# Gated cross-attention and top-2 expert layer on one core: tile phases from five, six and eight groups, tiles of 256 and 128 rows, and an earlier opening

## What is computed

```
x = x + tanh(g_xattn) * attention(layernorm(x), ctx, ctx, Wq..bo, mask)     # 16 heads of 8
x = x + tanh(g_ffn)   * experts(layernorm(x))

experts(x):                                   # 4096 rows
    scores    = x @ gate_w + gate_b           # 8 experts
    p, e      = softmax of the top 2 scores
    h[e]      = relu(x @ w1[e] + b1[e])       # 128 -> 512
    y[e]      = h[e] @ w2[e] + b2[e]          # 512 -> 128
    out       = p[0] * y[e[0]] + p[1] * y[e[1]]
```

## Time and profile before

| | |
|---|---|
| runs shown | 463.8, 464.79, 465.64 us (median 464.79) |
| the profiled execution | 462.04 us, its span 460.2 us |
| mean granted TensorE clock | 0.951 |
| busy: PE, PE weight load, DVE, ACT, POOL | 403.7, 327.5, 284.3, 271.4, 273.6 us |
| DMA | 72.55 MB, mean 158 GB/s |

### The profile page before, as it was taken

How to read it: one execution, slowest core, us unless ns; L and a number is a source line. 1 busy time by engine, 2 the same in 40 slices (tenths; PEclk the granted TensorE clock), 3 DMA queues, 4 the chain that set the end, 5 groups by cost and what they waited for, 6 DMA issues and landing times.

```text
span 460.2 us, 12345 instructions
## 1 busy us (share of the span) xinstructions
PE 403.7 (88%) x4299; PEld 327.5 (71%) x4299; DVE 284.3 (62%) x1034; ACT 271.4 (59%) x824; POOL 273.6 (59%) x297
## 2 busy tenths in 40 slices
PE   1799999999999999999998759999959999999700
PEld 1466677778777777777775639998848999999700
DVE  2678796788887878888889533446403333333257
ACT  1388777878787878877785413444313444444244
POOL 8743365277797887987746603777774445555500
PEclk9999999999999999999999768999979999999955
DMA  3999999830000000000000183677385777776188
GB/s 79 232 317 412 413 411 335 157 64 22 25 13 28 19 13 27 14 25 26 15 25 20 43 257 114 214 230 236 116 245 177 226 229 226 228 234 206 78 261 292
DMA packets 48154, 72.55 MB, mean 158 GB/s; under 512 B 8053, under 2 KB 32637, under 8 KB 48093
## 3 DMA queue, kind: packets, MB, share of 16 engines
q1 hardware_dynamic: 43549, 62.32, 44.3%
q0 software_dynamic: 4544, 9.45, 5.7%
HBM read 41.83 MB, written 34.66 MB: 166 GB/s over the span
## 4 chain that ended last, share of the span: by engine, by line
PE 74%; DVE 6%; POOL 6%; DMA 5%; issue 3%; ACT 2%; SPq 2%; POOLq 0%; ACTq 0%; DVEq 0%
PE U L747 8%; PE S L769 7%; PE S L635 7%; PE T L747 7%; PE O L769 7%; PE S L645 6%; PE O L675 6%; PE T L653 5%; PE O L685 5%; PE U L653 5%; POOL zs L996 3%; PE E L627 2%; DMA yg<-res 2%; ACT P L841 2%; PE E L616 2%
## 5 line engine op out<-in xcount | busy, mean ns | idle before, releaser
L841 ACT ACTIVATE P<-S,nmax 128x120 f32<-128x120 f32 x512 | 137.1, 413 | 41.0 <-DVE nmax L1137 41.0
L1007 POOL DMA_INDIRECT res<-yo,dpos x78 | 74.7, 957 | 75.8 <-DVE yo L1307 67.3
L1137 DVE TENSOR_REDUCE nmax<-S 128x4 f32<-128x480 f32 x128 | 75.2, 650 | 20.1 <-PE S L645 15.0
L996 POOL DMA_INDIRECT zs<-z,posu x64 | 64.6, 1009 | 36.4 <-PE O L685 15.5
L884 ACT ACTIVATE H<-U,wbuf 128x256 f32<-128x256 f32 x82 | 34.4, 470 | 53.9 <-PE U L747 53.8
L635 PE MATMUL S<-mb_r,I_r 128*128 128x480 f32 x128 | 61.7, 486 | 4.4 <-ACT P L841 3.9
L884 ACT ACTIVATE H<-T,wbuf 128x256 f32<-128x256 f32 x74 | 31.0, 470 | 51.5 <-PE T L747 51.5
L969 POOL TENSOR_SCALAR Kb<-Kt,hm 128x480 f32<-128x480 f32 x32 | 47.3, 1486 | 19.8 <-ACT Kt L868 6.9
L957 POOL TENSOR_SCALAR z<-X,mv,rstd 128x128 f32<-128x128 f32 x64 | 50.4, 793 | 10.9 <-PE O L685 7.1
L747 PE MATMUL U<-zT,wbuf 128*128 128x256 f32 x164 | 45.4, 402 | 1.6 <-ACT H L884 1.6
L747 PE MATMUL T<-zT,wbuf 128*128 128x256 f32 x148 | 39.6, 391 | 7.3 <-DMA wbuf<-wpk 5.2
(11 more groups left out here) (166 smaller groups left out, 693.5 us busy)
## 6 DMA issues: line engine op xcount, KB each, us to landing
wbuf<-wpk SPq DMA_DIRECT2D x39, 578.0 KB
zs<-zero SPq DMA_DIRECT2D x1, 17952.0 KB, 60.4
zin<-zs SPq DMA_DIRECT2D x39, 132.0 KB, 3.4
yg<-res SPq DMA_DIRECT2D x16, 256.0 KB, 3.7
wpk<-in_w SPq DMA_DIRECT2D x1, 2048.0 KB, 56.4
wpk<-in_w SPq DMA_DIRECT2D x8, 256.0 KB, 8.8
out<-X SPq DMA_DIRECT2D x16, 128.0 KB, 3.4
ctx_sb<-in_ctx SPq DMA_DIRECT2D x1, 1440.0 KB, 17.0
```

Source lines behind the costliest of these rows:

```text
L841: ins = nc.scalar.activation(P[:, n % 4, j, :], a[:, j * LK:(j + 1) * LK], ACT.Exp, bias=nmax[:, n % 4, j:j + 1])
L996: nc.gpsimd.indirect_dma_start(out=zs, out_offset=bass.IndirectOffsetOnAxis(ap=posu[:, F, k, i:i + 1], axis=0), in_=z2[:, F % 2, i, :], in ...
L1007: nc.gpsimd.indirect_dma_start(out=res, out_offset=bass.IndirectOffsetOnAxis(ap=dpos[:, n % NDP, h:h + 1], axis=0), in_=yo[:, n % NYO, h, ...
L1137: v.tensor_reduce(nmax[:, n % 4, :], Sb[n % NHG][:, 0:HG * LK].rearrange("p (j k) -> p j k", j=HG), AX_X, ALU.max, negate=True).then_inc(m ...
```

## The change

- `SB` becomes (5, 1, 2): tables are made after five, six and eight groups. The first phase has 12 tiles, the second 4, the third 15, and a fourth has `SINGLES` = 9 tiles of 128 rows. That is 31 tiles of 256 rows and 9 of 128, 71 halves. Rows that an expert has over its full tiles of 256 go to a tile of 256 or of 128.
- `tile_order` puts two tiles of 128 rows behind every three of the third phase. For a tile of 128 rows `first_product` computes all four chunks for its 128 rows.
- The stage is one sequence without an opening per phase. It opens in round 31 (`OPEN`), before the values of that round; the steps use banks S0 and S1 in turn, the first products T and U in turn.
- `DRAIN_PAIRS`: rounds 32 to 37 hold 4, 3, 3, 2, 2, 2 halves; 16 halves are placed.
- POOL scatters groups 5, 6 and 7 in rounds 31/32, 34 and 37, and results one round later.
- Six weight buffers. Rows and weights of the first 16 tiles are loaded without waiting for the last group.
- The start: loads are split over more semaphores, the first context is loaded earlier, z1 of group 0 and three of four masked keys move from POOL to DVE, V, tanh, b2 and bo move behind the first scores, into round 0.

```diff
-SB = (6, 2)
+SB = (5, 1, 2)
...
-NTB = [FULL, max((2 * NG * TOK + NE * (TS - 1)) // TS - FULL, (2 * SB[1] * TOK + 2 * NE * (TS - 1)) // TS)]
+FULL = [(2 * n * TOK - NE * (TS - 1)) // TS for n in LAST[:-1]]
+HS = 128
+SINGLES = NE + 1
+PAIRED = ((2 * NG * TOK + NE * (HS - 1)) // HS - SINGLES + 1) // 2
+NTB = [n - b for n, b in zip(FULL + [PAIRED], [0] + FULL)] + [SINGLES]
...
-NW = 4
+NW = 6
...
-DRAIN_PAIRS = {32: 4, 33: 4, 34: 4, 35: 4, 36: 4, 37: 4}
+DRAIN_PAIRS = {32: 4, 33: 3, 34: 3, 35: 2, 36: 2, 37: 2}
...
+def tile_order():
+
+    pairs = NTB[NB - 1]
+    run = -(-pairs // ((SINGLES + 1) // 2))
+    order, single = [(b, i) for b in range(NB - 1) for i in range(NTB[b])], 0
+    for i in range(pairs):
+        order.append((NB - 1, i))
+        if i % run == run - 1:
+            two = range(single, min(single + 2, SINGLES))
+            order += [(NB, c) for c in two]
+            single += len(two)
+    return order + [(NB, c) for c in range(single, SINGLES)]
...
+    subs, k, j = {}, B, 0
+    while j < SUBS and k < NR:
+        n = 2 * DRAIN_PAIRS.get(k, PAIRS)
+        subs[k] = list(range(j, min(j + n, SUBS)))
+        j, k = j + n, k + 1
+    return subs
...
-            return Sb[0] if late_step(m) else Ob
+            return Sb[m % 2]
...
+            for n in range(NT):
+                ahead = FULL[-1] if ROUND_OF.get(2 * HALF0[n + 1] - 1, NEVER) <= GB * (NG + 1) + 1 else NT
+                while z_next < min(n + NZ, ahead) or w_next < min(n + NW, ahead):
...
-                if k in PRE:
-                    for i, _ in OPENING:
-                        y_step(PRE[k], i)
...
                 if new:
                     scores(k + 1)
-
+                if k == OPEN:
+                    for i, _ in OPENING:
+                        y_step(i)
...
-                    F, n = (G - 3, 2 * GB - 4 + 2 * p) if p < 2 else (G - 2, 2 * (p - 2))
-                    if F == NG - 2:
-                        half(F, n)
-                        half(F, n + 1)
...
+                    if k == B:
+                        behind_sums(k)
+                        for n in range(2, 2 * GB):
+                            half(G - 3, n)
+                    elif k == B + 1:
+                        rows(G - 1)
+                    elif k == B + 2:
+                        for n in range(2 * GB):
+                            half(G - 2, n)
+                    elif k == B + 5:
+                        for part in range(GB):
+                            scatter(G - 2, part, GB)
+                for j in PLAN.get(k - 1, []) + (PLAN[k] if k == NR - 1 else []):
                     if j % 2:
-                        scatter_out(b, j // 2)
+                        scatter_out(j // 2)
...
+            dve.wait_ge(rstd1_done, 2)
+            for i in range(GB):
+                ins = v.tensor_scalar(z1[:, i, :], batch_x(0, i), mv1[:, 0, i, 0:1], rstd1[:, 0, 1, i:i + 1], ALU.subtract, ALU.mult)
+            ins.then_inc(z1_done, 1)
```

More of the change, by code:

```diff
@@ L68 @@
 NYO = 10
-NDP = NYO + 4
+NDP = NYO + 6
 TRASH = 2 + NDP * TS
@@ new lines, with halves @@
+TILES = tile_order()
+NT = len(TILES)
+def halves(n):
+    return UNIT[TILES[n][0]] // HS
+HALF = [(n, r) for n in range(NT) for r in range(halves(n))]
+NH2 = len(HALF)
+HALF0 = [HALF.index((n, 0)) for n in range(NT)] + [NH2]
+SUBS = 2 * (NH2 + TH)
+def round_plan():
+    subs, k, j = {}, B, 0
[4 more added lines that the diff above has]
+    return subs
+PLAN = round_plan()
+OPEN = B - 1
@@ L121, in rows_in @@
         return dict(OPENING)[i]
[L122 removed]
+    return (i + LEAD,) if i + LEAD < NH2 else ()
 def rows_out(i):
     return i - TH if i >= TH else None
[L130 to L139 removed]
@@ L142 @@
-LATE_STEP = min(m for m, key in enumerate(STEPS) if step_round(*key) >= LATE_ROUND)
-LATE_U = min(TH * N0[b] + i for b in range(NB) for i in range(TH * NTB[b]) if ROUND_OF.get((b, 2 * i), NEVER) >= LATE)
-def late_step(m):
-    return m >= LATE_STEP and (m - LATE_STEP) % 2 == 0
-def late_u(a):
-    return a >= LATE_U and (a - LATE_U) % 2 == 0
-def prior(n, late):
-    return max([m for m in (n - 1, n - 2) if m >= 0 and late(m) == late(n)], default=None)
-def tile_of(n):
-    b = max(b for b in range(NB) if N0[b] <= n)
-    return b, n - N0[b]
@@ L167, in rows_of, with chunks @@
-def rows_of(q):
-    b, i = tile_of(q // TH)
-    return b, TH * i + q % TH
+def chunks(i):
+    n, r = HALF[i]
+    each = NC // halves(n)
+    return range(r * each, (r + 1) * each)
+ZT_THROUGH = [sum(1 for i in STEPS[:m + 1] if rows_in(i)) for m in range(len(STEPS))]
+YO_THROUGH = [sum(1 for i in STEPS[:m + 1] if rows_out(i) is not None) for m in range(len(STEPS))]
+H_THROUGH = [sum(len(chunks(i)) for i in range(a + 1)) for a in range(NH2)]
+STEP_OF_ROWS = {q: m for m, i in enumerate(STEPS) for q in rows_in(i)}
@@ L173, in in_u @@
+def late_u(a):
+    return a % 2 == 0
 def in_u(n):
@@ L486, in y_bank, with sent, stored, table_ready @@
         def y_bank(m):
-            return Sb[0] if late_step(m) else Ob
-        def stored(eng, tiles):
+            return Sb[m % 2]
+        def sent(r, n):
+            return 16 * sum(halves(m) for m in range(r, n, NYO))
+        def stored(eng):
             for r in range(NYO):
-                wait(eng, y_out[r], 16 * TH * ((tiles - r + NYO - 1) // NYO))
+                wait(eng, y_out[r], sent(r, NT))
+        def table_ready(eng, ph):
+            eng.wait_ge(table_step, NTAB * (ph + 1))
+        def zt_part(q):
+            return zT[:, q // 2 % 2, q % 2 * HS:q % 2 * HS + HS]
+        def h_part(q):
+            return slice(q % 2 * HS, q % 2 * HS + HS)
         def unit_x(u):
@@ L1011, in half @@
             def half(F, n):
-                if 0 <= F < NG and F + 1 not in LAST:
+                if 0 <= F < NG - 1:
                     scatter(F, n, 2 * GB)
@@ L1122, in stats @@
             def stats(stat, mv, G, step):
+                wait(dve, step, at(G, 2, 0))
                 for i in range(GB):
```

464 lines of the change are left out of this document (221 added, 243 removed).

## The result

The changed kernel took **441.93 us** (median of 4 runs, 439.13 to 443.24), beside 464.84 for the kernel before: a ratio of 0.950, interval 0.9445 to 0.9555. It is 5% faster, by 22.9 us, where 33.8 were forecast. The number is 0.9 us above the range. That is less than the spread of the four runs, so what has to be explained is the 10.9 us between 431 and 441.93, not the edge of the range. The profiled execution took 439.13 us with a span of 437.3; it is the fastest of the four, with a mean granted clock of 0.97 against 0.952 to 0.962, so 2.8 us of the median aren't in this profile. In what follows medians are over all runs of a kernel, while the ratios leave out the runs that lie over 1.5% above the fastest of their kernel.

A forecast was written before the change was run, and what follows sets the result against it. PE was taken to bound the kernel, with DVE near it in attention. The terms summed to -32.4 us, giving 429.6 from the profiled execution or 432.4 from the median; 431 us was taken, range 423 to 441.

The forecast's parts named there:

- Fewer halves: Expert stage: 71 halves instead of 78 at 1.866 us each, -13.1 us; 128-column first products add 0.2.
- First rows early: Opening of the expert stage: the first product follows round 31's sums without waiting for rows, -4.5 us.
- The slow start: First halves of the expert stage: products alternate between two banks, so half 3 follows half 0 sooner, -5.7 us.
- Idle before tile 14 or so: PE's stop of 1.79 us before 323.07, put down to SP's queue at a boundary, goes: -1.8 us.
- The second dip: Expert stage around 334 us: the wait for the last group's rows is hidden, -9.2 us.
- Shorter rounds: Rounds 35 to 37 hold two halves, so the last group's chain is less covered, +2.5 us.
- One table more: Rounds 25 and 26: 4.6 us of added DVE work against its slack, with a smaller second table, +2.5 us.
- Start-up: Kernel start: earlier first scores, with batch 1's row maxima at 25.5 us, -3.3 us.
- the signs that the prediction set for being wrong: Observations that would contradict the forecast, among them scores of batch 1 starting later than 24 us.
- The tail: End of the kernel: 25 us without PE, which the change leaves alone.
- the late group: Rival: POOL's last-group operations slip and tile 16 waits, so the second dip's 9.2 comes back, 440 us; chance 0.14.
- the feed: Rival in the mixed tiles: 226 to 236 GB/s is a ceiling, some 4.5 groups lose 10 us, 441; chance 0.10.

The follow-up runs named there:

- no_singles: The changed kernel without tiles of 128 rows, so 39 tiles of 256 and 78 halves; 485.98 us on slower chips, ratio 1.0076 to the kernel before.
- spread37_b: The changed kernel with the table parts and weights of round 37 spread on DVE over the first seven steps after the rounds; 435.51 us, ratio 0.9387.
- short_pauses: The changed kernel with POOL fills of 0.65 us behind every second scatter from round 34 to step 60; 442.01 us, ratio 0.9492.
- thin_tables_b: The changed kernel with the first table's parts in rounds 26 to 28 and the second's in rounds 32 to 34 on DVE; 432.72 us, ratio 0.9354.
- nw4_b: The changed kernel with four weight buffers instead of six; 455.74 us, ratio 0.9803 to the kernel before.
- stats_later_b: The changed kernel with first-layernorm statistics of group 1 behind batch 1's row maxima and groups 2 to 7 one round later; 440.56 us, ratio 0.9502.
- paused: The changed kernel with a 2.2 us POOL fill behind every third scatter from round 34 to step 28; 470.33 us on slower chips, ratio 0.9765.

## Why the prediction was right or wrong

The direction and most terms held. Each term as the profiled execution has it, against the profile of the kernel before:

- *Fewer halves*, -13.1: right (no_singles: 13.4 between profiles). The first products of 128 columns cost nothing that shows, as the earlier trace rows had it: in the change a first product of eight such records starts at 347.09 and the next at 348.98, 1.89 us for the half. The Trainium skill (TensorE: Matmul & The Clock Gate, "The mechanism" of Part 3) says that a weight load overlaps running matmuls only when its row group differs, though the same section also lets one run ahead that goes to a background buffer. By the first rule alone, with the 107 ns per load of that page's "LDWEIGHTS", the half would have taken 0.43 us more, an estimate; the 1.89 us of the trace don't agree with it.
- *First rows early*, -4.5: -7.3 from the scores of batch 31 to the first product (11.23 us, before 18.49). I left the low clock before the last sums where it was, and in this profile it did not come. That is luck of the profile: in spread37_b and short_pauses, which have the same code up to there, the granted clock was at 1.2 GHz for 6.8 us from 260 us on, and the stretch took 13.52 and 13.39 us, so -5.0.
- *The slow start*, -5.7: -5.3 (4.2 against 9.5 us). Right.
- *Idle before tile 14 or so*, -1.8: **the step that failed**. I put the stop of 1.79 us before 323.07 down to SP's queue, because it stood at a boundary, without asking what DVE did ahead of the copy of `zT`. It was DVE's slots and table. DVE in the kernel before, where all from 318.12 on stands ahead of the copy that the product of 323.07 reads:

```profile
318.12 0.27 DVE L1218 TENSOR_TENSOR pm<-hot,pe 128x64 f32<-128x64 f32 x1
...
322.23 0.34 DVE L1262 TENSOR_REDUCE stf<-imul 128x23 f32<-128x184 f32 x1
...
322.68 0.28 DVE L1301 COPY zT<-S 128x128 f32<-128x128 f32 x1
```

The change has it again, larger, with 3.21 us and 1.7 of low clock behind it: round 37 holds two halves instead of four, so the table's last part no longer stands behind another copy but ahead of this one. That is 4.9 us where the forecast had none, +3.1 against the kernel before in place of -1.8, and spread37_b takes the stop away by order alone.
- *The second dip*, -9.2: right. POOL's last rows were scattered at 317.52 (forecast 316.8), SP issued their load at 321.56 (319), and PE had no wait for them.
- *Shorter rounds*, +2.5: +3.1 (1.08 and 2.04), right.
- *One table more*, +2.5: +4.2 between the scores of batches 25 and 31, 4.1 of it in the two rounds with the first table. The size of the work was right (DVE was busy for 4.8 us more in them, forecast 4.6); what failed is the overlap. I set it against DVE's slack in two windows of 7.3 us, but a burst has to fit where it stands: PE waited 1.00 us before 217.72 and 1.94 before 227.56, both times for ACT's probabilities, which wait for DVE's maxima. A third such wait, 1.72 us before 251.06, is no loss of the change: the kernel before has it too, before 247.27. With both tables spread over three rounds each the stretch takes 45.85 us, 0.3 more than in the kernel before (thin_tables_b).
- *Start-up*, -3.3: -0.4 in this profile, up to -1.9 in others. What failed is the 25.5 for the row maxima of batch 1: I had named the work ahead of them but counted one set of statistics where the queue has two, 2.6 us behind a wait for bo until 24.77. One of the signs that the prediction set for being wrong came with it: the scores of batch 1 start at 24.66, later than 24.
- *The tail*, at nothing: +1.5. From the start of the last second product to the end of the span are 27.8 us, and 26.5 to 28.5 in other profiles with the same code there; both profiles of the kernel before have 26.3. So part of it is scatter, and why the rest is longer stays open.

Measured against forecast, 2.9 us were lost at the start, 1.7 at the tables, 4.9 at the stop, 1.5 at the tail, 0.6 in the shorter rounds and 0.4 at the slow start, less 2.8 at the opening: 9.2 of the 9.5 us by which this execution (439.13) missed the 429.6 of the sum. The time is close to the rivals' 440 and 441, but only in number: neither the late group nor the feed, each priced at 9 to 10, cost anything. The range failed because its upper end came from those rivals, each at one place, and not from three DVE terms being wrong together. Two edits that only reorder DVE reach 432.7 and 435.5 us. That one of them lands where the sum (432.4) had put the change is a coincidence, since it keeps the stop and the late start.

The feed rival was worth its place: nw4_b shows it real for four buffers, and buffers five and six, which I costed at nothing, are what the small tiles live on.

## What to carry to other kernels

When an engine in order feeds the bound engine, don't compare its work with its slack per round: look for bursts, and lay each part behind the copy or maximum that somebody waits for. A stop marked "issue" at a boundary has an owner; follow the operand that the stopped instruction reads before giving it to the queue that changes there. And when tiles get smaller, count the buffers in time (weights per tile against microseconds per tile), since the transfer stays as large as before.

## What the hardware did that was not expected

- A wait of PE of some 2 to 3 us was at times, not always, followed by a granted clock of 1.2 GHz. The stop of 3.21 us behind round 37 had 3.4 us of it behind it in the change (1.7 us lost) and none in thin_tables_b. The wait of 1.92 us in round 27 had 6.8 us of it in stats_later_b (3.4 lost, 2.1 of them in that round); the same wait of 1.94 us in the change had none. Such waits can cost more than double what they show.
- On three of the chips, under trains of 10 to 19 scatters of POOL without a pause, ACT and DVE went on up to 16 us behind the recorded end of PE's products in the unedited change (18 in paused), which cost the change 16 us at one place and the kernel before less. There the change gains 2.2% instead of 5%. On the others a train of 55 did nothing of the kind.
- Under the fills of POOL in paused, operations of DVE that take 0.2 us took 3.0, each until a fill had ended.
